# A graph attention layer: one row vector of exponents spread through device memory, and layer normalisation moved to ScalarE

## The chip, the cores and the metric

One core of a Trainium2 chip runs the kernel. The metric is the device time of one execution in microseconds (us), the lower the better. The median of three runs of the kernel before is 437.91 us (437.85 to 437.98). In what follows PE is TensorE, DVE is VectorE, ACT is ScalarE, POOL is GpSimd and SP is SyncE, as the profile writes them.

## The reference

The input is x (4096 nodes, 256 features) and a 4096 x 4096 integer adjacency matrix.

```
h   = relu(layernorm(x))               # over the 256 features, eps 1e-5
h   = h @ W1 + b1                      # 256 x 256
e   = leaky_relu((h @ a1)[:, None] + (h @ a2)[None, :] + b2, 0.2)
att = softmax(where(adj > 0, e, -1e12), axis=1)
out = x + elu(att @ h)
```

## The kernel before

Nodes are cut into 32 tiles of 128. With r from `h @ a1` and p from `h @ a2`, the exponential of the leaky ReLU is, up to a factor of the row that the softmax cancels and a factor u of the column, `max(exp(r), exp(p))`. So the weight of an edge is `adj * max(R, p)`, where R, a row of 4096 values, is needed in the same form in all 128 partitions. Everything is fp32, split for PE into a high and a low part in its fp32r format.

**The head** makes h and its two products. It runs over 8 groups (`GROUPS`) of 4 tiles (`GT`). For a group g:

- DVE takes the statistics of x (`statistics`), POOL forms mean and variance (`moments`), ACT the root (`root`), DVE the reciprocal and the shift (`invert`).
- ACT normalises tiles 0 and 1 of the group and DVE tiles 2 and 3 (`normalise` on both engines, `NORM_ACT = 2`) into `xn`.
- PE transposes the group's 8 blocks into PSUM banks 0 and 1 (`transposes`); ACT applies the ReLU and writes `hnT` (`relu_T`, two halves kc); DVE forms the low part `hnT_lo` from the same banks (`low_T`). The transposes of group g wait for `low_T` of group g - 1, because they write the same banks.
- PE projects with 24 matmuls into banks 2 to 5 (`project`), DVE adds the bias and keeps `h_raw` (`keep_h`, two halves), POOL takes the exponents of r and p from two extra columns into `cr` and `cp` (`exponents`, it raises `c_ready`).
- For R, ACT repeats the four columns of `cr` along the free axis (`repeat_s1`), PE transposes them into bank 6 or 7 (`spread`), so that every partition holds the row, ACT copies them to R (`keep_s`) and later exponentiates 1024 columns of R in place, once for each chunk (`exp_R`).

Each engine runs its own queue in the order written out by hand. ACT's order in iteration g is `relu_T(g+1)`, `normalise(g+2)`, `root(g+3)`, `repeat_s1(g-1)`, `keep_s(g-2)`, with `sign` of pair 1 in iteration 2, the first Exp (of p, and R of chunk 0) in iteration 6 and `high` of pair 0 in iteration 7. DVE's is `invert(g+2)`, `low_T(g+1)`, `normalise(g+2)`, `statistics(g+4)`, `keep_h(g)`, with the sum of hnT (`hsum`, `hsrep`) and `mask(0, 0, 0)` ahead of the last `keep_h`. PE's is `transposes(g)`, `project(g-1)`, `spread(g-2)`.

Then follows **the end phase**: DVE takes the maximum of h @ a2 over all nodes, PE turns it and spreads it (bank 1, then `H0`), ACT forms `u`, and then scales and rounds the tiles of h (`hp_begin`, `scale_h`, `round_h`), with `keep_s(6)` and `keep_s(7)` among them.

**The stream.** Four chunks of 1024 output nodes, in each 16 pairs of source tiles, in rounds of 4 slots. For a pair ACT takes the sign of the adjacency (`sign`, L379), DVE multiplies it with max(R, p) (`mask`, L731), ACT makes the high part `w_hi` (`high`, L387), DVE the low part `w_lo` (`low`, L741), and PE runs 32 matmuls with w_hi and then 16 with w_lo into eight PSUM banks (L600, L602). SP loads one adjacency tile of 1 MB into a slot when its `w_lo` is done. Before the first pair PE opens the sum of each bank with one small matmul (`start_sum`, L576). At the end of a chunk ACT empties the banks, and the output is formed beside the next chunk.

Of the kernel before, what the change touches and what calls it, by code (L numbers as in the profile page):

```python
# [32 lines left out]
P = 128  # L33
# [10 lines left out]
GT = 4  # L44
GROUPS = TILES // GT
NORM_ACT = 2
# [34 lines left out]
def build(nc, adj_t, x, W1, vectors, out):  # L81
# [8 lines left out]
    with ctx:  # L90
# [28 lines left out]
        s1rep = over("s1rep", [P, 2, GT, P], fp32, e_s)  # L119
# [31 lines left out]
        cr = sb("cr", [P, TILES])  # L151
        cp = sb("cp", [P, TILES])
# [3 lines left out]
        H0, S0 = 2, 6  # L156
# [14 lines left out]
        s1_ready = sem("s1_ready")  # L171
# [3 lines left out]
        xn_ready = sem("xn_ready")  # L175
# [5 lines left out]
        s_ready = sem("s_ready")  # L181
        s_kept = sem("s_kept")
# [10 lines left out]
        R_ready = sem("R_ready")  # L193
# [135 lines left out]
        def _(act):  # L329
# [9 lines left out]
            def normalise(g):  # L339

                act.wait_ge(rstd_ready, g + 1)
                if g >= 2:
                    act.wait_ge(tp_ready, KC * (g - 1))
                for t in range(NORM_ACT):
                    tile = g * GT + t
                    last = act.activation(xn[:, g % 2, t, :], x_s[:, tile, :], ACT.Identity,  # L346
                                          scale=rstd[:, tile:tile + 1], bias=shift[:, tile:tile + 1])
                last.then_inc(xn_act, 1)

            def relu_T(g):  # L350

                if g >= 2:
                    act.wait_ge(h_ready, 2 * (g - 1))
                for kc in range(KC):
                    act.wait_ge(tp_ready, KC * g + kc + 1)
                    act.activation(hnT[:, g % 2, kc, :], ps[:, kc, :], ACT.Relu,
                                   accum_out=hs[:, kc, g:g + 1]).then_inc(hn_ready, 1)

            def repeat_s1(g):

                if g >= 2:
                    act.wait_ge(s_ready, g - 1)
                act.wait_ge(c_ready, g + 1)
                act.activation(s1rep[:, g % 2, :, :],
                               cr[:, g * GT:(g + 1) * GT].unsqueeze(2).broadcast_to([P, GT, P]),
                               ACT.Copy).then_inc(s1_ready, 1)

            def keep_s(g):
                act.wait_ge(s_ready, g + 1)
                act.activation(R[:, g * GT * P:(g + 1) * GT * P], ps[:, S0 + g % 2, :], ACT.Copy).then_inc(s_kept, 1)  # L370

            def exp_R(ic):
                part = R[:, ds(ic * CW, CW)]
                act.activation(part, part, ACT.Exp).then_inc(R_ready, 1)
# [22 lines left out]
            for g in range(GROUPS):  # L397
                if g + 1 < GROUPS:
                    relu_T(g + 1)
# [6 lines left out]
                if g >= 1:  # L406
                    repeat_s1(g - 1)
                if g == 6:
# [3 lines left out]
                    act.wait_ge(s_kept, CW // (GT * P))  # L412
                    exp_R(0)
                if g >= 2:
                    keep_s(g - 2)
# [4 lines left out]
            repeat_s1(GROUPS - 1)  # L420
# [39 lines left out]
            def round_of(ic, r, first, last):  # L460
                inner = r is not FIRST_ROUND and r is not LAST_ROUND
                for c in range(SLOTS):
# [14 lines left out]
                    if r is FIRST_ROUND and c == 2 and not last:  # L477
                        exp_R(ic + 1)
# [14 lines left out]
            keep_s(GROUPS - 2)  # L493
            keep_s(GROUPS - 1)
            act.wait_ge(s_kept, GROUPS)
# [10 lines left out]
        def _(pe):  # L506
            def transposes(g, u):

                pe.wait_ge(xn_ready, g + 1)
                pe.wait_ge(xn_act, g + 1)  # L510
                for kc in range(KC):
                    if at_least(g, 1):
                        pe.wait_ge(hn_lo_ready, (g - 1) * KC + kc + 1)
                    for t in range(GT):
                        last = pe.transpose(ps[:, kc, t * P:(t + 1) * P], xn[:, u, t, kc * P:(kc + 1) * P],  # L515
                                            ident[:, :])
# [16 lines left out]
            def spread(g, u):  # L533

                pe.wait_ge(s1_ready, g + 1)
                if at_least(g, 2):
                    pe.wait_ge(s_kept, g - 1)
                for t in range(GT):
                    last = pe.transpose(ps[:, S0 + u, t * P:(t + 1) * P], s1rep[:, u, t, :], ident[:, :])
                last.then_inc(s_ready, 1)  # L540

# [7 lines left out]
            spread(0, 0)  # L549
            transposes(3, 1)  # L550
            project(2, 0)
            spread(1, 1)
# [13 lines left out]
            spread(GROUPS - 2, 0)  # L566
# [11 lines left out]
            def pair(ic, m, b, first, begin=False):  # L578

                n = ic * PAIRS + m  # L580
                for part, w in ((0, w_hi), (1, w_lo)):
                    pe.wait_ge((hi_ready, lo_ready)[part], n + 1)
                    for s in range(2):
# [7 lines left out]
                        for ib in range(BANKS):  # L591
                            acc = ps[:, ib, 0:HW].unsqueeze(1)
                            block_w = w[:, b, s, ib * P:(ib + 1) * P]
                            if begin and part == 0 and s == 0 and not (first and ib < S0):
                                if first:
                                    pe.wait_ge(s_kept, GROUPS + ib - S0 - 1)
                                else:
                                    pe.wait_ge(evacuated, (ic - 1) * BANKS + ib + 1)
                                start_sum(ib)
# [34 lines left out]
            for ib in range(S0):  # L634
# [6 lines left out]
        def _(dve):  # L641
# [26 lines left out]
            def normalise(g):  # L668

                if g >= 2:  # L670
                    dve.wait_ge(tp_ready, KC * (g - 1))
                for t in range(NORM_ACT, GT):
                    tile = g * GT + t
                    last = dve.tensor_scalar(xn[:, g % 2, t, :], x_s[:, tile, :], mean[:, tile:tile + 1],  # L674
                                             rstd[:, tile:tile + 1], ALU.subtract, ALU.mult)
                last.then_inc(xn_ready, 1)

            def low_T(g):
# [3 lines left out]
                for kc in range(KC):  # L682
                    dve.wait_ge(hn_ready, KC * g + kc + 1)
                    dve.scalar_tensor_tensor(hnT_lo[:, g % 2, kc, :], ps[:, kc, :], 0.0,  # L684
# [62 lines left out]
            normalise(0)  # L747
            weights()
            invert(1)
            normalise(1)  # L750
# [5 lines left out]
            for g in range(GROUPS):  # L756
# [6 lines left out]
                if g + 2 < GROUPS:  # L763
                    normalise(g + 2)
# [7 lines left out]
                if g == 7:  # L772
# [7 lines left out]
                    dve.wait_ge(R_ready, 1)  # L780
# [48 lines left out]
            def round_of(ic, r, first, last):  # L829
                inner = r is not FIRST_ROUND and r is not LAST_ROUND  # L830
                for c in range(SLOTS):
# [10 lines left out]
                    if r is LAST_ROUND and c == 0 and not last:  # L842
                        dve.wait_ge(R_ready, ic + 2)
# [58 lines left out]
```

## Time and profile before

| | |
|---|---|
| median of 3 runs | 437.91 us |
| the profiled execution | 437.82 us |
| its span, first to last instruction | 436.0 us |
| PE busy | 413.6 us (95%), 3399 matmuls |
| DVE busy | 375.9 us (86%) |
| ACT busy | 315.9 us (72%) |
| POOL busy | 24.1 us (6%) |
| PE: L600 and L602, matmuls of the stream | 592.4 us as summed durations, which overlap |
| DMA | 80.60 MB, 185 GB/s on average |

The profile shows one execution. The busy share of an engine is an average over the head (to about 57 us), the stream and a short tail (from about 431 us). Durations of matmuls in a row overlap, so their pace is read from their start times or from a count in a stretch. ACT's and DVE's operations overlap their successors by about 0.1 us in the same way.

### The profile page before, as it was taken

How to read it: one execution, taken by the hardware profiler on the slowest of the kernel's cores; microseconds unless marked ns; L12 is line 12 of the kernel's file. 1: busy time of each engine (PE TensorE's matmuls, PEld its weight loads, DVE VectorE, ACT ScalarE, POOL GpSimd, SP SyncE). 2: the span in 40 equal slices, each digit the busy share in tenths (PEclk: the TensorE clock that was granted, in tenths of full speed). 3: DMA queues.
4: the chain of work that ended last, by engine and by line, in shares of the span. 5: the costliest groups of instructions: out<-in, count | busy, mean ns of one | idle time of the engine just before them, and what ended most of it. 6: DMA issues, size and time to landing. Idle time of an engine off the chain costs nothing.

```text
span 436.0 us, 8665 instructions
## 1 busy us (share of the span) xinstructions
PE 413.6 (95%) x3399; PEld 410.2 (94%) x3399; DVE 375.9 (86%) x403; ACT 315.9 (72%) x312; POOL 24.1 (6%) x95
## 2 busy tenths in 40 slices
PE   0799979999999999999999999999999999999995
PEld 0789979999999999999999999999999999999995
DVE  3999899999999389999996399999991799999905
ACT  2678899999996298958663799758562989576503
POOL 2333200000000000000000000000000000000005
PEclk9999999999999999999999999999999999999999
DMA  7940015555555725638478155747576256475302
GB/s 269 384 180 1 0 52 208 193 213 207 192 193 194 289 98 200 246 135 275 159 260 305 64 192 201 259 150 266 148 261 254 85 204 229 156 252 229 96 0 96
DMA packets 22355, 80.60 MB, mean 185 GB/s; under 512 B 1472, under 2 KB 14016, under 8 KB 14144
## 3 DMA queue, kind: packets, MB, share of 16 engines
q1 hardware_dynamic: 21920, 79.70, 51.6%
q10 hardware_dynamic: 416, 0.66, 0.5%
q8 instruction: 11, 0.18, 0.2%
q14 instruction: 8, 0.07, 0.0%
HBM read 76.15 MB, written 4.19 MB: 184 GB/s over the span
## 4 chain that ended last, share of the span: by engine, by line
PE 87%; DVE 8%; ACT 2%; DMA 2%; issue 1%; POOL 0%; POOLq 0%; SPq 0%; DVEq 0%; ACTq 0%
PE ps L600 52%; PE ps L602 26%; DVE stats L657 2%; DMA x_s<-x 2%; PE ps L618 1%; PE ps L616 1%; PE ps L617 1%; DVE hnT_lo L684 1%; PE ps L527 1%; DVE h_raw L693 1%; PE ps L529 1%; PE ps L528 1%; DVE y L878 1%; DVE xn L674 1%; PE ps L576 1%; PE ps L515 1%
## 5 line engine op out<-in xcount | busy, mean ns | idle before, releaser
L600 PE MATMUL ps<-hp_hi,w_hi 128*128 (+1 forms) x960 | 233.6, 282 | 0.9 <-ACT w_hi L387 0.9
L602 PE MATMUL ps<-hp_lo,w_hi 128*128 (+1 forms) x960 | 233.6, 282 | 0.0
L731 DVE SCALAR_TENSOR_TENSOR adj_s<-R,p,adj_s 128x1024 f32<-128x1024 f32 x128 | 158.2, 1276 | 31.7 <-ACT adj_s L379 31.7
L600 PEld LDWEIGHTS ps<-hp_hi,w_hi 128*128 128x128 f32 x960 | 181.3, 189 | 1.2 <-ACT w_hi L387 1.1
L602 PEld LDWEIGHTS ps<-hp_lo,w_hi 128*128 128x128 f32 x960 | 181.1, 189 | 0.0
L387 ACT ACTIVATE w_hi<-adj_s 128x2048 fp32r<-128x2048 f32 x64 | 122.4, 1913 | 33.5 <-DVE adj_s L731 33.0
L741 DVE SCALAR_TENSOR_TENSOR w_lo<-adj_s,w_hi 128x2048 fp32r<-128x2048 f32 x64 | 146.1, 2283 | 0.4 <-ACT w_hi L387 0.3
L379 ACT ACTIVATE adj_s<-adj_s 128x2048 f32<-128x2048 int32 x64 | 122.4, 1912 | 19.4 <-DMA adj_s<-adj_t 18.8
L600 PE MATMUL ps<-hp_hi,w_lo 128*128 (+1 forms) x960 | 125.2, 283 | 0.6 <-DVE w_lo L741 0.6
L600 PEld LDWEIGHTS ps<-hp_hi,w_lo 128*128 128x128 f32 x960 | 119.4, 189 | 0.8 <-DVE w_lo L741 0.8
L451 ACT ACTIVATE y<-ps 128x258 f32<-128x258 f32 x24 | 9.3, 387 | 28.1 <-PE ps L618 28.1
L326 POOL TENSOR_TENSOR adj_s<-y,adj_s 128x256 f32<-128x256 f32 x8 | 5.7, 709 | 373.0 <-DVE y L878 372.7
L515 PE MATMUL ps<-ident,xn 128*128 128x128 f32 x64 | 10.2, 312 | 13.7 <-ACT xn L346 11.2
L515 PEld LDWEIGHTS ps<-ident,xn 128*128 128x128 f32 x64 | 8.5, 161 | 14.4 <-issue 11.4
L527 PE MATMUL ps<-W_hi,hnT 128*128 128x258 f32 x64 | 19.7, 308 | 0.8 <-DVE h_raw L693 0.6
L529 PE MATMUL ps<-W_hi,hnT_lo 128*128 128x258 f32 x64 | 18.9, 295 | 0.0
L528 PE MATMUL ps<-W_lo,hnT 128*128 128x258 f32 x64 | 18.9, 295 | 0.0
L618 PE MATMUL ps<-hp_hi,w_lo 128*128 128x258 f32 x64 | 18.0, 282 | 0.0
L616 PE MATMUL ps<-hp_hi,w_hi 128*128 128x258 f32 x64 | 18.0, 281 | 0.0
L617 PE MATMUL ps<-hp_lo,w_hi 128*128 128x258 f32 x64 | 18.0, 281 | 0.0
L657 DVE BATCH_NORM_STATS2 stats<-x_s 128x6 f32<-128x256 f32 x32 | 11.2, 412 | 5.9 <-DMA x_s<-x 5.9
L503 ACT ACTIVATE y<-ps,rden 128x256 f32<-128x256 f32 x8 | 3.8, 475 | 15.9 <-DVE rden L867 15.9
(89 smaller groups left out, 273.9 us busy)
## 6 DMA issues: line engine op xcount, KB each, us to landing
adj_s<-adj_t SPq DMA_DIRECT2D x64, 1024.0 KB, 4.8
x_s<-x SPq DMA_DIRECT2D x8, 512.0 KB, 10.2
o_s<-x SPq DMA_DIRECT2D x3, 1024.0 KB, 7.7
out<-o_s SPq DMA_DIRECT2D x6, 512.0 KB, 6.9
adj_s<-x SPq DMA_DIRECT2D x1, 1024.0 KB, 5.5
out<-adj_s SPq DMA_DIRECT2D x8, 128.0 KB, 1.7
vec<-vectors ACTq DMA_DIRECT2D x1, 384.5 KB, 6.4
W1x<-W ACTq DMA_DIRECT2D x1, 256.0 KB, 4.8
```

Source lines behind the costliest of these rows:

```text
L379: act.activation(adj_w[:, c, :, :], adj_s[:, c, :, :], ACT.Sign).then_inc(signed, 1)
L387: act.activation(w_hi[:, c, :, :], adj_w[:, c, :, :], ACT.Relu).then_inc(hi_ready, 1)
L515: last = pe.transpose(ps[:, kc, t * P:(t + 1) * P], xn[:, u, t, kc * P:(kc + 1) * P], ident[:, :])
L527: pe.matmul(acc, hnT[:, u, kc, node], W_hi[:, kc, :], start=kc == 0, stop=False)
L528: pe.matmul(acc, hnT[:, u, kc, node], W_lo[:, kc, :], start=False, stop=False)
L529: last = pe.matmul(acc, hnT_lo[:, u, kc, node], W_hi[:, kc, :], start=False, stop=kc == KC - 1)
L600: last = pe.matmul(acc, block_w, hh, start=False, stop=False)
L602: pe.matmul(acc, block_w, hl, start=False, stop=False)
L616: pe.matmul(acc, w_hi[:, b, s, col], hh, start=False, stop=False)
L617: pe.matmul(acc, w_hi[:, b, s, col], hl, start=False, stop=False)
L731: last = dve.scalar_tensor_tensor(sgn, R[:, ds(ic * CW, CW)], p[:, ds(source(r, c) + s, 1)], sgn, ALU.max, ALU.mult)
L741: dve.scalar_tensor_tensor(w_lo[:, c, :, :], adj_w[:, c, :, :], 0.0, w_hi[:, c, :, :].bitcast(fp32), ALU.max, ALU.subtract).then_inc(lo_re ...
```

## The change

R is no longer built in 8 steps in all partitions. PE turns 16 columns of `cr` (128 x 16) into 16 rows of 128 with one transpose (`turn_r`, twice), ACT exponentiates these 16 x 128 values (`exp_r`), and SP stores them as 8 KB to a tensor in device memory and loads them back to all 128 partitions, 1 MB (`spread`, now on SP). `repeat_s1`, `keep_s`, `exp_R` and PE's `spread` are gone. The first half is turned on PE between `project(4)` and `transposes(6)`, and PE waits there for `exp_r(0)`, which ACT does at the start of iteration 5; the second half is turned beside the maximum. `mask(0, 0, 0)` waits for the load of the first half. ACT normalises all four tiles of a group, DVE none. The transposes use banks 0 and 1 for even groups and 6 and 7 for odd ones, and wait for `low_T` of group g - 2. The loop over groups on PE is written out, and all eight sums are opened ahead of the first pair.

```diff
-NORM_ACT = 2
+HALF_T = TILES // 2
...
-        s1rep = over("s1rep", [P, 2, GT, P], fp32, e_s)
...
+        r_row = [sb(f"r_row{k}", [HALF_T, P]) for k in range(2)]
+        r_rows = nc.dram_tensor("r_rows", (TILES, P), fp32, kind="Internal").ap()
...
-        H0, S0 = 2, 6
+        H0 = 2
+        T0 = (0, 6)
+        RB = (1, 6)
...
+            def spread(k):
+                tiles = slice(k * HALF_T, (k + 1) * HALF_T)
+                sp.wait_ge(r_ready, k + 1)
+                sp.dma_start(r_rows[tiles, :], r_row[k][:, :]).then_inc(r_out, 16)
+                sp.wait_ge(r_out, (k + 1) * 16)
+                sp.dma_start(R[:, k * HALF_T * P:(k + 1) * HALF_T * P],
+                             r_rows[tiles, :].rearrange("t p -> (t p)").partition_broadcast(P)).then_inc(R_in, 16)
+            spread(0)
+            spread(1)
...
-                for t in range(NORM_ACT):
+                for t in range(GT):
                     tile = g * GT + t
                     last = act.activation(xn[:, g % 2, t, :], x_s[:, tile, :], ACT.Identity,
...
-                    act.activation(hnT[:, g % 2, kc, :], ps[:, kc, :], ACT.Relu,
+                    act.activation(hnT[:, g % 2, kc, :], ps[:, T0[g % 2] + kc, :], ACT.Relu,
...
-            def repeat_s1(g):
-            def keep_s(g):
-            def exp_R(ic):
...
+            def exp_r(k):
+                act.wait_ge(rT_ready, k + 1)
+                act.activation(r_row[k][:, :], ps[0:HALF_T, RB[k], 0:P], ACT.Exp).then_inc(r_ready, 1)
...
             for g in range(GROUPS):
+                if g == 5:
+                    exp_r(0)
                 if g + 1 < GROUPS:
                     relu_T(g + 1)
...
-                if g >= 1:
-                    repeat_s1(g - 1)
                 if g == 6:
                     act.wait_ge(c_ready, EARLY // GT)
                     act.activation(p[:, 0:EARLY], cp[:, 0:EARLY], ACT.Exp).then_inc(p_ready, 1)
-                    act.wait_ge(s_kept, CW // (GT * P))
-                    exp_R(0)
-                if g >= 2:
-                    keep_s(g - 2)
...
-            repeat_s1(GROUPS - 1)
+            exp_r(1)
+            act.wait_ge(c_ready, GROUPS)
             act.activation(p[:, EARLY:TILES], cp[:, EARLY:TILES], ACT.Exp).then_inc(p_ready, 1)
...
-                    if r is FIRST_ROUND and c == 2 and not last:
-                        exp_R(ic + 1)
...
-            keep_s(GROUPS - 2)
-            keep_s(GROUPS - 1)
-            act.wait_ge(s_kept, GROUPS)
...
-                pe.wait_ge(xn_ready, g + 1)
                 pe.wait_ge(xn_act, g + 1)
                 for kc in range(KC):
-                    if at_least(g, 1):
-                        pe.wait_ge(hn_lo_ready, (g - 1) * KC + kc + 1)
+                    if at_least(g, 2):
+                        pe.wait_ge(hn_lo_ready, (g - 2) * KC + kc + 1)
...
-            def spread(g, u):
...
+            def turn_r(k):
+                pe.wait_ge(c_ready, (k + 1) * HALF_T // GT)
+                pe.transpose(ps[0:HALF_T, RB[k], 0:P], cr[:, k * HALF_T:(k + 1) * HALF_T], ident[:, :]).then_inc(rT_ready, 1)
...
-            with pe.Fori(2, GROUPS // 2) as k:
+            for k in range(2, GROUPS // 2):
                 transposes(2 * k, 0)
                 project(2 * k - 1, 1)
-                spread(2 * k - 2, 0)
                 transposes(2 * k + 1, 1)
                 project(2 * k, 0)
-                spread(2 * k - 1, 1)
+                if k == 2:
+                    turn_r(0)
+                    pe.wait_ge(r_ready, 1)
...
             pe.transpose(ps[0:1, 1, 0:P], gm[:, 0:1], ident[:, :]).then_inc(pmaxT_ready, 1)
+            turn_r(1)
             pe.wait_ge(g1_ready, 1)
             pe.matmul(ps[:, H0, 0:1], ones[0:1, 0:P], gm[0:1, 1:2], start=True, stop=True).then_inc(g_ps, 1)
-            spread(GROUPS - 1, 1)
...
             pe.wait_ge(prep_done, 1)
-            for ib in range(S0):
+            pe.wait_ge(r_ready, 2)
+            for ib in range(BANKS):
                 start_sum(ib)
...
-            def normalise(g):
...
-                    dve.wait_ge(R_ready, 1)
+                    dve.wait_ge(R_in, 16)
                     mask(0, 0, 0)
...
-                    if r is LAST_ROUND and c == 0 and not last:
-                        dve.wait_ge(R_ready, ic + 2)
+                    if first and r is LAST_ROUND and c == 0:
+                        dve.wait_ge(R_in, 32)
```

The first part of the diff is in `build`, then come SP's queue (`spread`), ACT's, PE's and DVE's.

## Rows read from the trace of the kernel before

**Rows 1.** Stretches: length, busy us of PE, PEld, DVE, ACT, POOL, clock, DMA share, GB/s.

```profile
30.00:40.00 10.00, 9.68 (x79) 8.99 (x78) 9.78 (x26) 9.15 (x22) 3.87 (x20) 1.00 0.00 1
...
70.00:430.00 360.00, 360.00 (x3007) 360.00 (x3006) 313.60 (x249) 263.97 (x212) 2.05 (x3) 1.00 0.55 193
...
433.00:436.00 3.00, 0.00 (x0) 0.00 (x0) 0.13 (x1) 0.00 (x0) 0.84 (x2) 0.68 0.39 131
```

**Rows 2.** Waits over the span: who for whom, total us, times, longest.

```profile
ACT hnT L356 <- PE ps L515: 5.1, 5, 1.5
```

**Rows 3.** Timeline, 11 to 23 us: start, length, operation, idle time before it.

```profile
11.93 0.30 ACT L336 ACTIVATE std<-var,eps 128x4 f32<-128x4 f32 x1 [0.85 <-POOL var L304]
...
13.76 0.57 ACT L356 ACTIVATE hnT<-ps 128x512 fp32r<-128x512 f32 x1
...
21.02 1.09 ACT L346 ACTIVATE xn<-x_s,shift,rstd 128x256 f32<-128x256 f32 x2 [1.70 <-DVE shift L665]
...
21.57 0.28 PE L529 MATMUL ps<-W_hi,hnT_lo 128*128 128x258 f32 x1
22.01 0.28 ACT L336 ACTIVATE std<-var,eps 128x4 f32<-128x4 f32 x1
...
22.20 1.07 PE L515 MATMUL ps<-ident,xn 128*128 128x128 f32 x8 [0.36 <-issue]
...
22.93 0.60 ACT L356 ACTIVATE hnT<-ps 128x512 fp32r<-128x512 f32 x1 [0.64 <-PE ps L515]
```

**Rows 4.** Timeline of VectorE, groups 2 and 3.

```profile
24.34 1.29 DVE L684 SCALAR_TENSOR_TENSOR hnT_lo<-ps,hnT 128x512 fp32r<-128x512 f32 x2
25.54 0.73 DVE L674 TENSOR_SCALAR xn<-x_s,mean,rstd 128x256 f32<-128x256 f32 x2
...
28.98 1.29 DVE L684 SCALAR_TENSOR_TENSOR hnT_lo<-ps,hnT 128x512 fp32r<-128x512 f32 x2
```

**Rows 5.** Timeline of ScalarE, 31 to 60 us.

```profile
31.28 1.90 ACT L379 ACTIVATE adj_s<-adj_s 128x2048 f32<-128x2048 int32 x1
33.08 0.58 ACT L356 ACTIVATE hnT<-ps 128x512 fp32r<-128x512 f32 x1
...
34.22 1.09 ACT L346 ACTIVATE xn<-x_s,shift,rstd 128x256 f32<-128x256 f32 x2
...
48.06 1.28 ACT L411 ACT_TABLE_LOAD   x1
49.35 0.22 ACT L411 ACTIVATE p<-cp 128x24 f32<-128x24 f32 x1
49.48 1.05 ACT L374 ACTIVATE R<-R 128x1024 f32<-128x1024 f32 x1
...
58.07 1.05 ACT L370 ACTIVATE R<-ps 128x512 f32<-128x512 f32 x2
```

**Rows 6.** Timelines of TensorE, VectorE and GpSimd, 45 to 66 us.

```profile
45.56 1.04 PE L515 MATMUL ps<-ident,xn 128*128 128x128 f32 x8
...
50.73 2.48 DVE L731 SCALAR_TENSOR_TENSOR adj_s<-R,p,adj_s 128x1024 f32<-128x1024 f32 x2
...
54.91 0.23 POOL L312 TENSOR_SCALAR cp<-h_raw 128x4 f32<-128x4 f32 x1
...
55.36 0.38 PE L571 MATMUL ps<-gm,ones 1*128 1x1 f32 x2 [0.37 <-DVE gm L787]
...
62.53 2.19 PE L600 MATMUL ps<-hp_hi,w_lo 128*128 128x258 f32 x16 [0.61 <-DVE w_lo L741]
...
65.59 0.39 PE L600 MATMUL ps<-hp_hi,w_hi 128*128 128x258 f32 x1 [0.86 <-ACT w_hi L387]
```

**Rows 7.** DMA issues: queue, number, KB of one, us from issue to landing.

```profile
adj_s<-adj_t SPq DMA_DIRECT2D x64, 1024.0 KB, 4.8
x_s<-x SPq DMA_DIRECT2D x8, 512.0 KB, 10.2
...
out<-adj_s SPq DMA_DIRECT2D x8, 128.0 KB, 1.7
```

More of the change, by code:

```diff
@@ L170, in build @@
         const_ready = sem("const_ready")
-        s1_ready = sem("s1_ready")
         var_ready = sem("var_ready")
@@ L174, in build @@
         xn_act = sem("xn_act")
-        xn_ready = sem("xn_ready")
         tp_ready = sem("tp_ready")
@@ L180, in build @@
         h_kept = sem("h_kept")
-        s_ready = sem("s_ready")
-        s_kept = sem("s_kept")
         hsrep_ready = sem("hsrep_ready")
@@ L192, in build @@
         u_ready = sem("u_ready")
-        R_ready = sem("R_ready")
+        rT_ready = sem("rT_ready")
+        r_ready = sem("r_ready")
+        r_out = sem("r_out")
+        R_in = sem("R_in")
         ones_col = sem("ones_col")
@@ L355, in relu_T @@
                     act.wait_ge(tp_ready, KC * g + kc + 1)
-                    act.activation(hnT[:, g % 2, kc, :], ps[:, kc, :], ACT.Relu,
+                    act.activation(hnT[:, g % 2, kc, :], ps[:, T0[g % 2] + kc, :], ACT.Relu,
                                    accum_out=hs[:, kc, g:g + 1]).then_inc(hn_ready, 1)
-            def repeat_s1(g):
-                if g >= 2:
[L362 to L366, printed above, removed]
-            def keep_s(g):
-                act.wait_ge(s_ready, g + 1)
-                act.activation(R[:, g * GT * P:(g + 1) * GT * P], ps[:, S0 + g % 2, :], ACT.Copy).then_inc(s_kept, 1)
-            def exp_R(ic):
-                part = R[:, ds(ic * CW, CW)]
-                act.activation(part, part, ACT.Exp).then_inc(R_ready, 1)
+            def exp_r(k):
+                act.wait_ge(rT_ready, k + 1)
+                act.activation(r_row[k][:, :], ps[0:HALF_T, RB[k], 0:P], ACT.Exp).then_inc(r_ready, 1)
             def sign(ic, r, c):
@@ L411, in _ @@
                     act.activation(p[:, 0:EARLY], cp[:, 0:EARLY], ACT.Exp).then_inc(p_ready, 1)
-                    act.wait_ge(s_kept, CW // (GT * P))
-                    exp_R(0)
-                if g >= 2:
-                    keep_s(g - 2)
                 if g == 7:
@@ L507, in transposes @@
             def transposes(g, u):
-                pe.wait_ge(xn_ready, g + 1)
                 pe.wait_ge(xn_act, g + 1)
                 for kc in range(KC):
-                    if at_least(g, 1):
-                        pe.wait_ge(hn_lo_ready, (g - 1) * KC + kc + 1)
+                    if at_least(g, 2):
+                        pe.wait_ge(hn_lo_ready, (g - 2) * KC + kc + 1)
                     for t in range(GT):
-                        last = pe.transpose(ps[:, kc, t * P:(t + 1) * P], xn[:, u, t, kc * P:(kc + 1) * P],
+                        last = pe.transpose(ps[:, T0[u] + kc, t * P:(t + 1) * P], xn[:, u, t, kc * P:(kc + 1) * P],
                                             ident[:, :])
@@ L531, in project @@
                         last.then_inc(h_ready, 1)
-            def spread(g, u):
[L535 to L540, printed above, removed]
             pe.wait_ge(pool_c, 3)
@@ L548, in _ @@
             project(1, 1)
-            spread(0, 0)
             transposes(3, 1)
             project(2, 0)
-            spread(1, 1)
-            with pe.Fori(2, GROUPS // 2) as k:
+            def turn_r(k):
+                pe.wait_ge(c_ready, (k + 1) * HALF_T // GT)
+                pe.transpose(ps[0:HALF_T, RB[k], 0:P], cr[:, k * HALF_T:(k + 1) * HALF_T], ident[:, :]).then_inc(rT_ready, 1)
+            for k in range(2, GROUPS // 2):
                 transposes(2 * k, 0)
                 project(2 * k - 1, 1)
-                spread(2 * k - 2, 0)
                 transposes(2 * k + 1, 1)
                 project(2 * k, 0)
-                spread(2 * k - 1, 1)
+                if k == 2:
+                    turn_r(0)
+                    pe.wait_ge(r_ready, 1)
             project(GROUPS - 1, 1)
@@ L565, in _ @@
             last.then_inc(hsum_ps, 1)
-            spread(GROUPS - 2, 0)
             pe.wait_ge(pmax_ready, 1)
             pe.transpose(ps[0:1, 1, 0:P], gm[:, 0:1], ident[:, :]).then_inc(pmaxT_ready, 1)
+            turn_r(1)
             pe.wait_ge(g1_ready, 1)
             pe.matmul(ps[:, H0, 0:1], ones[0:1, 0:P], gm[0:1, 1:2], start=True, stop=True).then_inc(g_ps, 1)
-            spread(GROUPS - 1, 1)
             def start_sum(ib):
@@ L593, in pair @@
                             block_w = w[:, b, s, ib * P:(ib + 1) * P]
[L594 to L598, printed above, removed]
+                            if begin and part == 0 and s == 0 and not first:
+                                pe.wait_ge(evacuated, (ic - 1) * BANKS + ib + 1)
                                 start_sum(ib)
@@ L666, in invert @@
                     .then_inc(rstd_ready, 1)
-            def normalise(g):
[L670 to L676, printed above, removed]
             def low_T(g):
@@ L683, in low_T @@
                     dve.wait_ge(hn_ready, KC * g + kc + 1)
-                    dve.scalar_tensor_tensor(hnT_lo[:, g % 2, kc, :], ps[:, kc, :], 0.0,
+                    dve.scalar_tensor_tensor(hnT_lo[:, g % 2, kc, :], ps[:, T0[g % 2] + kc, :], 0.0,
                                              hnT[:, g % 2, kc, :].bitcast(fp32), ALU.max, ALU.subtract)\
@@ L746, in _ @@
             invert(0)
-            normalise(0)
             weights()
             invert(1)
-            normalise(1)
             split_weights()
@@ L762, in _ @@
                     invert(2)
-                if g + 2 < GROUPS:
-                    normalise(g + 2)
                 if g + 4 < GROUPS:
```

## The prediction

> **What bounds the kernel now.** I read the stretches first [rows 1]. From 70 to 430 us TensorE is busy for 360.00 of 360.00 us, so nothing that relieves ScalarE or VectorE there can shorten the span, and the matmuls of that part are not changed. What can move is the moment at which the pair stream starts without a gap, which is the head. The head ends with two short gaps in front of the stream [rows 6]: 0.61 us until VectorE's w_lo at 62.53, 0.86 us until ScalarE's w_hi at 65.59. From 65.59 on TensorE never waits. So the question is: when does the matmul at 65.59 (pair 1, its w_hi part) start after the change? Everything behind it moves by the same amount.
>
> In the head, 30 to 40 us has VectorE at 9.78, TensorE at 9.68 and ScalarE at 9.15 of 10 us [rows 1]: all three are near full, so I follow the pitch of the groups. VectorE's low_T(2) starts at 24.34 and low_T(3) at 28.98, 4.64 us apart [rows 4], with no idle time of VectorE named in either row: VectorE sets the pace there. ScalarE has waits in between, 5.1 us in 5 times, all for the transposes [rows 2].
>
> **What the change takes away.** VectorE loses its two tiles of normalise, about 0.65 us of each group (0.73 for two overlapping [rows 4]); its pitch would be 3.99. TensorE loses four transposes a group and ScalarE two passes (repeat_s1, keep_s). In the end phase ScalarE loses keep_s(6) and keep_s(7), 1.05 us [rows 5], which lie between u and w_hi of pair 1. The exp_R passes of the later chunks lie beside a full TensorE: nothing. At the head of chunk 0, exp_R(0) (1.05 us [rows 5]) is beside VectorE's work and is not waited for: nothing.
>
> **What it adds, and where.** ScalarE now normalises four tiles, 1.98 instead of 0.99 us (21.02 to 22.01 for two [rows 3]), and it does so between relu_T(g+1) and the transposes of g+2, for which it then waits. That is a ring: transposes start; relu_T starts 0.73 us later (22.20 to 22.93 [rows 3]); relu_T takes 1.14 (33.08 to 34.22 [rows 5]); the transposes start 1.18 us after a two-tile normalise starts (21.02 to 22.20 [rows 3]), so 2.17 after a four-tile one. Sum 0.73 + 1.14 + 2.17 = 4.04 us. This is a hair above VectorE's 3.99, so ScalarE's ring becomes the pace, and nothing in it has slack: whatever else stands in ScalarE's queue there is paid in full.
>
> Entry. relu_T(0) starts at 13.76, right behind normalise(1) [rows 3]; two more tiles put it, and VectorE's low_T(0) that waits for it, 0.99 late. normalise(0) costs nothing more: its two further tiles fill a wait of 0.85 us in front of root(1) [rows 3] and end about when that starts. From there VectorE is without a gap until the shift that releases normalise(2) at 21.02 (nothing of what it does there is removed: its normalise(0) and (1) lie before low_T(0), normalise(2) behind that shift), so normalise(2) starts at 22.01 and the transposes of group 2 at 22.01 + 2.17 = 24.18 instead of 22.20 [rows 3]. The two new banks let transposes(1) start before low_T(0), but project(0) comes no earlier for that, since it needs all of low_T(0), which is late; and nothing waits for it, since TensorE will stand idle in front of the transposes of group 2: no gain, no loss.
>
> Then the ring. Group 3 at 28.22, group 4 at 32.26. In iteration 2 ScalarE also does sign of pair 1, 1.80 us [rows 5] (31.28 to 33.08), which before fell mostly into its waits. Now: normalise(4) from 28.22 + 0.73 + 1.14 = 30.09 to 32.08, root(5) 0.2, sign to 34.09, where relu_T(4) would otherwise start at 32.99: 1.1 us paid. Group 5: 34.09 + 1.14 + 2.17 = 37.40.
>
> Then exp_r(0). TensorE turns the first 16 columns after project(4) and waits for r_ready before the transposes of group 6. ScalarE's order is relu_T(5), normalise(6), root(7), then exp_r(0), and exp_r(0) is now the first Exp, so the table load that stood before the exponent of p (48.06, 1.28 us [rows 5]) stands here. normalise(6) runs from 39.27 to 41.26, root(7) ends 41.54 (0.28 as in [rows 3]), the load 42.82, exp_r(0) about 0.31 us (between 0.22 for 24 columns and 1.05 for 1024, 0.00083 us a column [rows 5]) to 43.13, and TensorE starts at 43.25. Without it group 6 would start at 37.40 + 4.04 = 41.44: 1.8 us paid. Whether the load comes before or after the wait matters little: turning is done at 41.3 + 0.3 = 41.6 and ScalarE reaches the load at 41.54. Group 7: 43.25 + 4.04 = 47.29, against 45.56 [rows 6]. From the relief of VectorE there is a gain of only 0.25 us between groups 2 and 7 (45.56 - 22.20 = 23.36 before, 47.29 - 24.18 = 23.11 after), because sign and exp_r(0) eat it. The head is 1.73 us late here.
>
> The Trainium skill, "ScalarE: Activation LUTs", section "What ACT_TABLE_LOAD costs", puts a switch of table sets at 1.28 us and another 1.38 us of drain. The trace has p's ACTIVATE at 49.35, 0.01 us behind the load's end [rows 5], so it shows no such drain; by the page the sum would be 1.4 us more.
>
> R through device memory. r_ready 43.2; a store of 8 KB, bounded by the 128 KB stores at 1.7 us; then 1 MB to 128 partitions, as the adjacency tiles, 4.8 us [rows 7]: R_in at about 49.9 with issue. Bounds: 0 for the store and 4.8, or 1.7 and 10.2 (the x loads while the queues were full [rows 7]), 48.0 to 55.2. mask(0,0,0) wants it at 50.73 + 1.73 = 52.46 [rows 6]. The queues carry 1 GB/s at 30 to 40 us [rows 1], so I take 4.8, the row of the same shape, 8 KB to each of 128 partitions: hidden with 2.6 us to spare. The second half is wanted by chunk 2 only; in SP's queue it stands ahead of load_adj(4), which waits for the same w_lo as TensorE at 62.53 [rows 6], 1.8 later; store and load are issued at 57.6 and over by about 64.3 (57.6 + 1.7 + 4.8 and the issue), so the tile isn't held up. Nothing.
>
> End phase. From the transposes of group 7 to mask(0,0,0), keep_h(7) and the maximum the order is unchanged, all 1.73 late. turn_r(1) now waits on TensorE for cp of POOL (ends 55.14) and is ahead of the matmul that spreads the maximum (55.36) [rows 6]: 0.2 us of room for an issue of 0.1 to 0.2, I take 0.05. exp_r(1) and the second p fit before u. Then ScalarE's way to w_hi of pair 1 is shorter by 1.05: 65.59 + 1.78 - 1.05 = 66.32. TensorE itself: w_lo of pair 0 at 62.53 + 1.78 = 64.31, and 16 matmuls of 0.12 (360 us for 3007 [rows 1]) to 66.23. The later of them, 66.32, is 0.73 after 65.59. Eight sums opened at once instead of six: same count, TensorE waits for w_lo there anyway.
>
> Sum: 1.98 (entry) - 0.25 (ring, with sign and the table load inside) + 0.05 - 1.05 = +0.73 us. The profiled execution took 437.82 us (span 436.0), 0.09 below the median of 437.91. 437.91 + 0.73 = 438.64; I say 438.6. About 0.2% (0.88 us, 437.03 to 438.79) is what a measurement of this kernel can tell from no change, and the sum lies just inside.
>
> **Rivals.**
> A. As worked: 438.1 to 439.2, from 0.2 to 0.3 us of error at each of entry, sign and exp_r. Chance 0.62.
> B. Faster: ScalarE's ring is not the pace. If a four-tile normalise let the transposes start tile by tile, or the latencies were shorter so that the ring fell under 3.99, VectorE's relief would count in the four groups that still have statistics: 4 x 0.65 = 2.6. With +1.0 at the entry, +1.4 for the table load and -1.05: 436.7; with the table load hidden too, 435.3. For it: VectorE is the pace now [rows 4], ScalarE shows waits [rows 2]. Against: these waits are the latency of the ring, not room, and xn_act is signalled once, after the fourth tile. It decides if the ring takes under 3.99 us. Chance 0.12.
> C. R is late: it decides once store and load take more than 9.2 us together. At the upper bound (55.2) mask(0,0,0) is 2.7 us late: 441.3. Chance 0.08.
> D. TensorE's clock falls. Between project(0), over by 21.6, and the transposes of group 2 it now stands idle for 2.6 us (0.4 before: 21.85 to 22.20 [rows 3]). The one fall that the trace has is behind the last matmul: the granted clock of 433 to 436 us is 0.68 on average [rows 1], so it went to 1.2 GHz within about 3 us of idleness. At the lower level project(1) takes up to twice its 24 matmuls of 0.12, 2.9 us, which holds back group 3: +1.5 to +2.7, so 440.1 to 441.3. Against it: 2.6 is less than that idleness. Chance 0.09.
> E. The page's drain behind the table load: the load in the ring costs 1.38 more, 440.0. Chance 0.02, since the row speaks against it.
> The rest, 0.07, is a wait of 0.3 to 1 us that I haven't seen.
>
> **Range and chances.** A alone reaches 438.1 to 439.2. To leave out no more than 2 in 10 I go down to 437.2 (into B) and up to 440.4 (into D, E and the nearer part of C). Slower by over 0.2%: a good third of A (its centre is 0.15 under the border), C, D, E and most of the rest: 0.43. Faster by over 0.2%: most of B, 0.10. Within: 0.47.
>
> **What would show it.** In the profile after: transposes of group 2 start near 24.2 with TensorE idle 2.6 us before them; groups 3 and 4 follow at 4.0 us; groups 4 to 5 at 5.1, 5 to 6 at 5.8 with a table load in front of exp_r(0) and TensorE waiting for it about 1.8 us; VectorE waits for ScalarE's hnT in each group; no wait of mask(0,0,0) for a transfer; the gap before w_hi of pair 1 nearly gone while the one before w_lo of pair 0 stays. Wrong if the groups follow at under 3.9 us, if mask waits for R, or if the matmuls of project(1) take clearly more than the 0.28 of [rows 3].

## The result and the profile after

The changed kernel takes 440.13 us (440.06 to 441.15, 4 runs), the kernel before 437.95 us beside it. The ratio is 1.0056, with a 95% interval of 1.0044 to 1.0068: slower by 2.2 us. I had said 438.6, slower by 0.7 us.

TensorE's timeline shows where the head lost it. The rows with x8 are the transposes of groups 2 to 7; the first and the last of them answer to the ones at 22.20 [rows 3] and 45.56 [rows 6] of the kernel before.

```profile
20.46 0.28 PE L522 MATMUL ps<-W_hi,hnT_lo 128*128 128x258 f32 x1
24.17 1.09 PE L508 MATMUL ps<-ident,xn 128*128 128x128 f32 x8 [3.43 <-ACT xn L360]
...
25.49 0.42 PE L520 MATMUL ps<-W_hi,hnT 128*128 128x258 f32 x1
...
29.50 1.04 PE L508 MATMUL ps<-ident,xn 128*128 128x128 f32 x8
...
33.48 1.09 PE L508 MATMUL ps<-ident,xn 128*128 128x128 f32 x8
...
38.59 1.09 PE L508 MATMUL ps<-ident,xn 128*128 128x128 f32 x8 [1.13 <-ACT xn L360]
...
44.40 1.09 PE L508 MATMUL ps<-ident,xn 128*128 128x128 f32 x8 [1.73 <-ACT r_row L376]
...
48.44 1.09 PE L508 MATMUL ps<-ident,xn 128*128 128x128 f32 x8
```

Group 2 starts at 24.17 us, against the 24.18 that I had worked out. But TensorE has then been idle for 3.43 us, not 2.6, and the matmuls of project(1) behind it change from 0.28 us at 25.22 to 0.42 us at 25.49. Group 3 follows 5.33 us after group 2 instead of 4.04. Groups 3 to 7 keep to the sum: 3.98, 5.11 (with sign), 5.81 (with the table load and exp_r(0)), 4.04. Group 7 starts at 48.44; I had 47.29.

The stretches of the same execution (columns as in [rows 1], the clock is the figure after the engines' counts):

```profile
20.00:25.00 5.00, 1.57 (x15) 1.36 (x14) 4.73 (x14) 2.63 (x7) 2.62 (x15) 1.00 1.02 424
25.00:29.00 4.00, 4.00 (x23) 4.00 (x22) 3.19 (x7) 3.34 (x9) 1.16 (x7) 0.57 0.37 152
29.00:59.00 30.00, 25.02 (x199) 23.27 (x197) 22.48 (x54) 20.38 (x46) 9.02 (x39) 1.00 0.10 37
...
60.00:63.00 3.00, 3.00 (x15) 3.00 (x15) 3.00 (x4) 2.97 (x7) 0.00 (x0) 0.51 0.66 259
```

The granted clock is 0.57 on average from 25 to 29 us and 0.51 from 60 to 63 us. So TensorE went to 1.2 GHz twice before the stream ran full, the first time behind its 3.43 us of idleness, the second time at the eight sums (`h_tiny`) that open pair 0. From 29 to 59 us it had 2.4 GHz.

ScalarE's rows bear out the terms that concern it: relu_T(0) at 14.78 (14.75 worked out), the table load of 1.28 us in front of exp_r(0), and 0.27 us for exp_r.

```profile
14.78 0.57 ACT L370 ACTIVATE hnT<-ps 128x512 fp32r<-128x512 f32 x1
...
42.78 1.28 ACT L376 ACT_TABLE_LOAD   x1
44.08 0.27 ACT L376 ACTIVATE r_row<-ps 16x128 f32<-16x128 f32 x1
```

R was no problem. The issues (KB of one, us to landing), SP's issues and VectorE's first mask are:

```profile
R<-r_rows SPq DMA_DIRECT2D x2, 1024.0 KB, 4.5
...
r_rows<-r_row SPq DMA_DIRECT2D x2, 8.0 KB, 1.3
```

```profile
45.74 0.34 SPq L259 DMA_DIRECT2D R<-r_rows  x1
...
60.08 0.32 SPq L259 DMA_DIRECT2D R<-r_rows  x1
65.48 0.34 SPq L235 DMA_DIRECT2D adj_s<-adj_t  x1
```

```profile
53.65 2.47 DVE L706 SCALAR_TENSOR_TENSOR adj_s<-R,p,adj_s 128x1024 f32<-128x1024 f32 x2
```

The first load is issued at 45.74, 1.39 us after the end of exp_r(0), and lands some 4.5 us later, at about 50.3. mask(0,0,0) starts at 53.65 without a wait. The second load is issued at 60.08; the adjacency load behind it in SP's queue follows at 65.48, over 5 us later, so it is not held up by it.

The end phase, first the kernel before (TensorE's timeline), then the changed one:

```profile
53.51 0.60 PE L539 MATMUL ps<-ident,s1rep 128*128 128x128 f32 x4
...
55.92 0.66 PE L539 MATMUL ps<-ident,s1rep 128*128 128x128 f32 x4 [0.19 <-ACT s1rep L364]
```

```profile
57.63 0.27 PE L556 MATMUL ps<-ident,gm 128*1 128x128 f32 x1 [1.48 <-DVE gm L756]
...
59.69 2.09 PE L563 MATMUL ps<-h_tiny,ones 128*128 128x258 f32 x8 [0.99 <-DVE h_tiny L770]
...
66.02 2.08 PE L584 MATMUL ps<-hp_hi,w_lo 128*128 128x258 f32 x16
```

Before, the old spreads of R (0.60 and 0.66 us) lay ahead of the maximum and behind it. In the changed kernel TensorE is idle for 1.48 and 0.99 us there, and the eight sums of h_tiny behind the second gap take 2.09 us. w_lo of pair 0 is used from 66.02 on, where before it was 62.53 [rows 6], and there is no gap in front of it, because TensorE had not finished with w_hi.

### The profile page after: what moved, and what is told of

Its sections match the earlier page's. It is cut to its first block, busy times and chain, and to the rows that moved or that the text cites. A ratio compares the mean times of both kernels' runs of the same rounds, so it can differ in the third digit from the quotient of the medians.

```text
span 438.3 us, 8557 instructions
## 1 busy us (share of the span) xinstructions
PE 411.1 (94%) x3369; PEld 408.4 (93%) x3369; DVE 371.1 (85%) x387; ACT 312.3 (71%) x310; POOL 24.1 (6%) x95
## 4 chain that ended last, share of the span: by engine, by line
PE 87%; ACT 5%; DVE 4%; DMA 2%; issue 1%; POOL 0%; POOLq 0%; SPq 0%; ACTq 0%; DVEq 0%
PE ps L584 53%; PE ps L586 26%; ACT xn L360 3%; DMA x_s<-x 2%; PE ps L600 1%; PE ps L602 1%; PE ps L601 1%; ACT hnT L370 1%; PE ps L508 1%; PE ps L563 1%; DVE stats L642 1%; DVE y L849 1%; PE ps L522 1%; DVE hnT_lo L659 1%; PE ps L520 1%
## 5 line engine op out<-in xcount | busy, mean ns | idle before, releaser
L360 ACT ACTIVATE xn<-x_s,shift,rstd 128x256 f32<-128x256 f32 x32 | 16.6, 594 | 3.2 <-DVE shift L650 3.2
L659 DVE SCALAR_TENSOR_TENSOR hnT_lo<-ps,hnT 128x512 fp32r<-128x512 f32 x16 | 10.3, 685 | 7.1 <-ACT hnT L370 6.1
```

## The experiments

All of them take the changed kernel as their base, apart from one. A filling is a row of transposes of the identity into a PSUM bank that nobody reads at that time; it adds nothing to the result. All fillings use this function:

```diff
+            def fill(bank, n):
+                for _ in range(n):
+                    pe.transpose(ps[:, bank, 0:P], ident[:, :], ident[:, :])
```

**The gap before group 2 filled.**

```diff
             project(0, 0)
+            fill(0, 24)
             transposes(2, 0)
```

> The changed kernel with 24 more 128x128 transposes of the identity into bank 0 between project(0) and transposes(2); they add nothing to the result. Clock theory: the 1.3 us by which group 3's transposes came later than the worked 4.04 us behind group 2's is TensorE at 1.2 GHz, after 3.4 us of idleness. With the gap filled the clock stays at 2.4 GHz, groups 2 to 3 are 4.0 to 4.1 us apart, and the time falls by 1.2 us to about 438.9. Rival (ring only: ScalarE's four-tile normalise sets the pace whatever TensorE's clock is): groups 2 to 3 stay at about 5.3 us, time 440.1 as before. If the 24 transposes themselves are in the way, the transposes of group 2 start later than 24.17 us.

Measured: 439.58 us (438.68 to 440.64, 7 runs), ratio 1.0033 (1.0022 to 1.0045). In the profiled execution, the slowest of the seven, groups 2 to 3 are 28.11 - 24.07 = 4.04 us apart and group 7 starts at 47.08, so the first fall is gone, as the clock theory says, and the rival fails. The time fell by 0.55 us in the median and not by 1.2. Most of the difference lies outside the span, the time from the first instruction to the last. The median span fell from 438.3 to 437.1 us, which is the 1.2. But these runs take 2.0 to 2.8 us beyond their span, and those of the changed kernel and of the kernel before 1.7 to 1.9. Why, no run shows. The second fall still comes, and in the profiled execution it is longer than in the changed kernel's:

```profile
25.00:30.00 5.00, 4.92 (x43) 4.71 (x42) 4.36 (x11) 4.38 (x13) 2.00 (x11) 1.00 0.30 120
...
55.00:60.00 5.00, 2.52 (x11) 2.13 (x12) 4.02 (x13) 4.30 (x9) 0.64 (x3) 0.74 0.09 26
60.00:65.00 5.00, 5.00 (x28) 5.00 (x28) 5.00 (x5) 5.00 (x8) 0.00 (x0) 0.58 0.45 185
```

**The gaps of the end phase filled.**

```diff
             last.then_inc(hsum_ps, 1)
+            fill(7, 18)
...
             pe.matmul(ps[:, H0, 0:1], ones[0:1, 0:P], gm[0:1, 1:2], start=True, stop=True).then_inc(g_ps, 1)
+            fill(7, 8)
```

> The changed kernel with 18 transposes of the identity into bank 7 behind the matmuls of hsum and 8 behind the one that spreads the maximum. Clock theory: the granted clock, 0.50 from about 59.8 to 63.0 us, stays at 1.00, the first matmuls of pair 0 follow at 0.12 instead of 0.21 us, pair 1 starts 0.3 to 0.6 us earlier, time about 439.7. Rival (pair 1 is bound by ScalarE's and VectorE's chain from u, so TensorE's clock under pair 0 costs nothing): 440.1.

Measured: 441.23 us (439.92 to 441.31, 4 runs), ratio 1.0077 (1.0060 to 1.0093). Both theories missed: one run is at 439.9 and three are at 441.2 to 441.3. The profiled execution is the fastest of the four. Its clock holds from 55 us on, but it falls at the first gap, and earlier than in the changed kernel. TensorE was idle for 2.56 us there and already has 1.2 GHz when the transposes of group 2 start (1.97 us for the eight, and a clock of 0.50):

```profile
24.02 1.97 PE L508 MATMUL ps<-ident,xn 128*128 128x128 f32 x8 [2.56 <-ACT xn L360]
```

```profile
24.00:25.00 1.00, 0.97 (x5) 0.98 (x6) 0.62 (x3) 0.16 (x1) 0.85 (x5) 0.50 1.00 418
25.00:30.00 5.00, 5.00 (x36) 5.00 (x35) 3.80 (x8) 3.55 (x10) 1.52 (x9) 0.78 0.29 118
...
55.00:60.00 5.00, 4.81 (x37) 4.05 (x36) 3.76 (x12) 3.15 (x6) 0.64 (x3) 1.00 0.01 2
```

The three slower runs have no trace, only their mean granted clock over the span: 0.989 to 0.992, against 0.995 for the profiled one. The changed kernel has such a run too (441.15, with 0.988 against 0.992 for its other three). More time at 1.2 GHz may go with them, but the mean alone does not show it: the kernel before has means of 0.993 to 0.999 in runs of 437.8 to 438.4 us. Also, 18 transposes were too many: they ended after the maximum was ready, and held TensorE's work on it back by 0.3 us.

**Both filled.** The two edits together.

> Both fillings in one kernel. Clock theory: the gains add, 1.2 + 0.4, time 438.4 to 438.6, which is the sum that was worked out for the change without any fall of the clock. Rival (ring only): 440.1. If the second fall is one consequence of the first (its gap moved with it), the gain is that of the first filling alone, 438.9.

Measured: 438.91 us (438.80 to 439.10, 10 runs), ratio 1.0023 (1.0014 to 1.0033). The scatter of 1 to 2 us is gone as well. It is 0.3 us above the upper end of what was expected, as much as the filling that was too long costs; the next experiment tests that.

**The fillings fitted.** 24, 12 and 8 transposes.

> The changed kernel with its three gaps of TensorE filled by 24, 12 and 8 transposes of the identity; the middle filling is six shorter than in the first such kernel, where it held the maximum back by 0.3 us. It tests the worked sum of the prediction by itself, without any fall of the clock: 0.73 us above the kernel before, so 438.5 to 438.8. If the sum was wrong in its own terms and two errors hid each other, the time is outside 438.3 to 439.0.

Measured: 438.59 us (438.45 to 438.80, 11 runs), the kernel before 437.89 beside it, ratio 1.0016 (1.0007 to 1.0025): 0.70 us slower, against a worked sum of 0.73. TensorE's rows, groups 2 to 7 and then w_lo of pair 0:

```profile
24.21 1.09 PE L508 MATMUL ps<-ident,xn 128*128 128x128 f32 x8 [0.82 <-ACT xn L360]
...
28.24 1.09 PE L508 MATMUL ps<-ident,xn 128*128 128x128 f32 x8
...
32.28 1.09 PE L508 MATMUL ps<-ident,xn 128*128 128x128 f32 x8
...
37.39 1.09 PE L508 MATMUL ps<-ident,xn 128*128 128x128 f32 x8 [1.14 <-ACT xn L360]
...
43.19 1.09 PE L508 MATMUL ps<-ident,xn 128*128 128x128 f32 x8 [1.72 <-ACT r_row L376]
...
47.22 1.09 PE L508 MATMUL ps<-ident,xn 128*128 128x128 f32 x8
```

```profile
64.29 2.18 PE L592 MATMUL ps<-hp_hi,w_lo 128*128 128x258 f32 x16 [0.76 <-DVE w_lo L724]
```

The steps are 4.03, 4.04, 5.11, 5.80 and 4.03 us. Worked out were 24.18, 28.22, 32.26, 37.40, 43.25 and 47.29 for the groups and 64.31 for w_lo.

**Two tiles on VectorE again.** `normalise` is back on both engines for each group; R and the four banks stay changed.

```diff
+def on_act(g):
+    return GT // 2
...
-                for t in range(GT):
+                for t in range(on_act(g)):
...
+            def normalise(g):
+                if on_act(g) == GT:
+                    return
+                if g >= 2:
+                    dve.wait_ge(tp_ready, KC * (g - 1))
+                for t in range(on_act(g), GT):
+                    tile = g * GT + t
+                    last = dve.tensor_scalar(xn[:, g % 2, t, :], x_s[:, tile, :], mean[:, tile:tile + 1],
+                                             rstd[:, tile:tile + 1], ALU.subtract, ALU.mult)
+                last.then_inc(xn_ready, 1)
```

> One part of the change undone: VectorE normalises tiles 2 and 3 of every group again, ScalarE tiles 0 and 1; R still goes through device memory and the transposes keep four banks. Theory (four tiles in ScalarE's ring cause both the late entry and the gap in which the clock falls): transposes of group 2 at 22.2 us, VectorE the pace at 4.64 us a group, group 7 at 45.4 to 45.8, exp_r with its table load nearly hidden, pair 1 at about 64.4 to 64.9, time 436.7 to 437.3, faster than the kernel before by the two copies of R that have left the end phase. Rival (the loss is exp_r and the wait of TensorE for it in the middle of the groups): group 5 to 6 stays at 5.8 us and the time at 438.5 or more.

Measured: 437.12 us (436.62 to 438.14, 10 runs), ratio 0.9987 (0.9977 to 0.9996). Group 2 starts at 22.44, groups 3 to 5 follow 4.4 to 4.7 us apart and group 6 5.36 us behind group 5, TensorE waits 0.46 us for exp_r(0) instead of 1.73, and group 7 starts at 45.35. So the four tiles in ScalarE's queue are the loss, and exp_r alone is not. The clock holds behind a gap of 2.02 us in front of group 2 and falls in the end phase:

```profile
22.44 1.07 PE L516 MATMUL ps<-ident,xn 128*128 128x128 f32 x8 [2.02 <-DVE xn L669]
```

```profile
25.00:30.00 5.00, 4.35 (x37) 4.14 (x37) 4.97 (x14) 2.91 (x9) 2.37 (x13) 1.00 0.30 121
...
55.00:60.00 5.00, 4.02 (x21) 3.81 (x22) 4.42 (x12) 4.42 (x11) 0.00 (x0) 0.66 0.37 152
```

**The same with the end phase filled** (12 and 8 transposes).

> The kernel with two tiles each on ScalarE and VectorE (R through device memory, four banks), and 12 and 8 transposes of the identity into bank 7 in TensorE's two gaps of the end phase. In the kernel without them the granted clock of 55 to 60 us was 0.66. Clock theory: it stays at 1.00, pair 1 starts 0.3 to 0.6 us earlier, 436.5 to 436.7, and the runs scatter less. Rival (TensorE's clock there costs nothing, the chain behind u decides): 437.1 with the same scatter.

Measured: 436.66 us (436.51 to 436.72, 7 runs), ratio 0.9969 (0.9957 to 0.9980), with a scatter of 0.2 instead of 1.5 us (on another chip than the run without fillings, beside 437.99 and 437.93 of the kernel before). The clock theory holds here too, and the gap of 2.33 us in front of group 2, which is not filled, is not followed by a fall:

```profile
22.20 1.07 PE L516 MATMUL ps<-ident,xn 128*128 128x128 f32 x8 [2.33 <-DVE xn L676]
```

```profile
55.00:60.00 5.00, 5.00 (x41) 4.79 (x42) 4.42 (x9) 4.63 (x11) 0.00 (x0) 1.00 0.40 156
```

**Only the normalisation moved, in the kernel before.**

```diff
-NORM_ACT = 2
+NORM_ACT = 4
...
-                pe.wait_ge(xn_ready, g + 1)
                 pe.wait_ge(xn_act, g + 1)
```

VectorE's `normalise` and its calls are gone.

> One part of the change done alone in the kernel before: ScalarE normalises all four tiles; R is still built with repeat_s1, spread and keep_s, and the transposes have two banks. Ring theory: ScalarE's queue per group is 1.14 + 1.98 + 0.2 + 0.52 + 0.48 = 4.3 us with no room, group 2 at 24.2, group 7 near 47.7, which is 2.1 late; with a fall of the clock in the gap before group 2 another 0.5 to 1.3 us. Time 440.0 to 441.4. Rival (the loss comes from the new way of R: its table load, its waits): time within 0.5 us of the kernel before, since VectorE is relieved.

Measured: 443.48 us (443.42 to 444.20, 4 runs), ratio 1.0131 (1.0114 to 1.0148). The direction was right, but the size was not: 5.5 us instead of 2 to 3.5 over the kernel before (437.99 beside it). Groups 2 to 3 take 5.23 us and 3 to 4 take 5.18, with the clock at 1.00 in both:

```profile
24.12 1.09 PE L514 MATMUL ps<-ident,xn 128*128 128x128 f32 x8 [1.56 <-ACT xn L346]
...
28.86 0.66 PE L538 MATMUL ps<-ident,s1rep 128*128 128x128 f32 x4 [0.76 <-ACT s1rep L364]
29.35 1.04 PE L514 MATMUL ps<-ident,xn 128*128 128x128 f32 x8
...
34.03 0.66 PE L538 MATMUL ps<-ident,s1rep 128*128 128x128 f32 x4 [0.77 <-ACT s1rep L364]
34.53 1.04 PE L514 MATMUL ps<-ident,xn 128*128 128x128 f32 x8
```

TensorE waits 0.76 us for s1rep in front of the old spread, and the transposes of the next group stand behind that in its queue. repeat_s1 comes behind ScalarE's normalise. So here the ring is 0.75 (transposes to relu_T) + 1.16 (relu_T) + 1.97 (normalise) + 0.19 (root) + 0.67 (repeat_s1, to the start of the old spread) + 0.49 (from there to the transposes) = 5.23 us, from the start times of this trace. I had added up ScalarE's queue alone, 4.3 us, and left out the legs over TensorE. From group 2 to group 7 it takes 51.20 - 24.12 = 27.08 us, against 23.36 before: 3.72. With 1.92 at the entry that is 5.64, and the profiled executions are 443.42 - 437.82 = 5.60 us apart. In the end phase the clock falls in this execution too (0.50 from 63 to 65 us), behind gaps of 0.60, 0.37 and 0.19 us, the same as in the trace of before, where it stayed up. It costs nothing there: w_hi of pair 1 follows 71.17 - 51.20 = 19.97 us behind group 7, and 20.03 before.

**sign of pair 1 out of the ring**, in the changed kernel with the fitted fillings.

```diff
                 if g == 6:
                     act.wait_ge(c_ready, EARLY // GT)
                     act.activation(p[:, 0:EARLY], cp[:, 0:EARLY], ACT.Exp).then_inc(p_ready, 1)
+                    sign(0, 0, 1)
...
-                if g == 2:
-                    sign(0, 0, 1)
```

> The changed kernel with four tiles on ScalarE, TensorE's gaps filled (24, 12 and 8 transposes of the identity), and sign of pair 1 moved from iteration 2 to behind the first exponent of p in iteration 6, where ScalarE was idle for 5.6 us. Ring theory (whatever stands in ScalarE's queue between two groups is paid in full): groups 4 to 5 go from 5.10 to 4.04 us and the time falls by 1.1 us from 438.6 (the kernel with fillings, less the 0.3 us by which its filling was too long) to 437.5. Rival (VectorE's 3.99 us a group takes over, so that the gain is cut to less than half): 438.1 or more.

Measured: 437.62 us (437.50 to 437.73, 10 runs), ratio 0.9991 (0.9982 to 1.0001). That is 0.97 us less than the 438.59 of the fitted kernel (the two ran on different chips, beside 437.99 and 437.89 of the kernel before; measured from these it is 0.37 us faster against 0.70 slower, 1.07 in all). Groups 4 to 5 take 4.03 us:

```profile
32.34 1.09 PE L507 MATMUL ps<-ident,xn 128*128 128x128 f32 x8
...
36.37 1.09 PE L507 MATMUL ps<-ident,xn 128*128 128x128 f32 x8
...
42.18 1.09 PE L507 MATMUL ps<-ident,xn 128*128 128x128 f32 x8 [1.73 <-ACT r_row L376]
```

**Tiles split by group.** `on_act(g)` is 4 for groups 3, 4 and 5 and 2 for the others; sign as above; 12 and 8 transposes in the end phase.

> Two tiles on ScalarE in groups 0, 1, 2, 6 and 7, four in groups 3, 4 and 5; sign of pair 1 in iteration 6; 12 and 8 transposes of the identity in the end phase. Ring theory: group 2 at 22.4 us with no gap before it, then about 4.04 us a group instead of 4.64, group 7 near 43.5, time 434.6 to 435.4. Rival (VectorE stays the pace because its work for the first two groups and the bias keeps it behind): group 7 at 45 or later, 436.3 or more.

Measured: 435.68 us (434.85 to 436.48, 4 runs), ratio 0.9941 (0.9922 to 0.9960), in two pairs: 434.9 and 436.5. The profiled execution is of the slower pair. TensorE was idle for 2.45 us before group 2 at 22.36, where I had expected no gap, and group 3 follows 5.94 us later:

```profile
22.36 1.06 PE L515 MATMUL ps<-ident,xn 128*128 128x128 f32 x8 [2.45 <-DVE xn L675]
...
28.30 1.04 PE L515 MATMUL ps<-ident,xn 128*128 128x128 f32 x8
```

```profile
25.00:30.00 5.00, 5.00 (x34) 5.00 (x34) 3.85 (x11) 2.87 (x8) 2.38 (x13) 0.73 0.31 128
```

**The same with the first gap filled** (`fill(0, 12)`).

> The version that the other runs point to: two tiles on ScalarE in groups 0, 1, 2, 6, 7, four in 3, 4, 5; sign of pair 1 in iteration 6; R through device memory; 12, 12 and 8 transposes of the identity in TensorE's gaps. The same kernel without the first filling came out at 434.9 or at 436.5, with groups 2 to 3 5.9 us apart and the clock at 0.73 from 25 to 30 us in a run of the slower kind. Clock theory: every run at 434.8 to 435.2, groups 2 to 3 at 4.3 to 4.5 us. Rival (the two levels have another cause than the clock in that gap): the runs stay spread between 434.9 and 436.5.

Measured: 434.62 us (434.58 to 434.78, 5 runs), ratio 0.9927 (0.9913 to 0.9941), 3.3 us faster than the kernel before. All five runs are together, 0.02 to 0.22 us below the expected 434.8; the step between groups 2 and 3 is 4.45 us. So the two levels came from this gap.

```profile
22.18 1.06 PE L515 MATMUL ps<-ident,xn 128*128 128x128 f32 x8 [1.06 <-DVE xn L676]
...
26.63 1.04 PE L515 MATMUL ps<-ident,xn 128*128 128x128 f32 x8
```

## Why the prediction was wrong

- **The step that failed** is the treatment of rival D. The sum took TensorE's clock as given, and "2.6 is less than that idleness" was the reason for a chance of 0.09. The trace after shows the clock fall behind that gap, and the filling shows that the gap was the cause. The time lay 2.18 us above the kernel before, 1.45 more than the sum's 0.73. Filling the gaps gives 1.54 back (440.13 to 438.59) and leaves 0.70. Rival D had the mechanism, but the time within its 440.1 to 441.3 is in part luck: it priced the first fall alone at 1.5 or more, which measured 1.2, and it had no second fall.
- **Two things in that step were off.** The first is the idle time, 3.43 and not 2.6 us (with the 21.85 of [rows 3] for the end of project(0) it would even have been 2.3). The matmuls of project(0) change from 0.42 to 0.28 us each at about 18.6 us, where in the trace of before they did so at 20.9, and so they ended at 20.7. The profile's clock column has 1.00 there in both traces, so that the lower pace at the start is seen in the matmuls alone. The second is the comparison. A gap of 2.56 us in front of group 2 was followed by 1.2 GHz with only the end phase filled, and one of 2.45 us in the mixed split, so the 2.6 us would have been no safety either. The single fall in the trace of before gave no lower bound for the idle time that it takes.
- **The price of each fall.** In the profiled executions the first fall puts group 7 at 48.44 instead of 47.22, 1.2 us later, and w_hi of pair 1 then comes at 67.94 instead of 66.39: 0.3 more from the second. The median spans say the same: 438.3 us with both, 437.1 with the first gap filled, 436.8 with all. But the second alone lasted longer in the profiled execution with the first gap filled, and w_hi of pair 1 came at 67.75 there, 20.67 us behind group 7 instead of 19.17: 1.5.
- **The second fall was not foreseen at all.** I had taken the old spreads of R off TensorE in the end phase and counted the room as free. Idle for 1.48 and 0.99 us there, TensorE opens pair 0 at 1.2 GHz: the eight sums of h_tiny take 2.09 us, and 1.23 with the gaps filled. With two tiles on each engine, filling these gaps alone is worth 437.12 - 436.66 = 0.46 us in the median, and up to 1.5 in single runs.
- **Entry: right.** 24.18 worked out, 24.17 measured. No gain from the two banks here: with the old banks and four tiles on ScalarE group 2 starts at 24.12.
- **The ring: right.** 4.04 worked out, 4.03 to 4.04 measured, and sign costs 1.07 in it (5.11 - 4.04; taken out, the time falls by 0.97). Rival B is out: VectorE's 3.99 never becomes the pace.
- **Table load and exp_r: right.** 5.80 against 5.85 worked out. The rival of a drain behind the load (the Trainium skill, "ScalarE: Activation LUTs", "What ACT_TABLE_LOAD costs") is out for this kernel: exp_r(0) starts at 44.08, 0.02 us behind the load's end at 44.06.
- **R through device memory: hidden**, with 3.3 us to spare (2.6 worked out; mask(0,0,0) was itself 1.2 us later than worked out). Rival C is out.
- **End phase: right in size.** w_lo of pair 0 at 64.29, worked out 64.31, once the clock stays up. As worked, pair 1 waits for TensorE's own 16 matmuls or for w_hi, which come within 0.1 us of each other.
- **What I did not see about the change as a whole:** its parts have opposite signs. The new way of R, together with the four banks, which no run takes apart, is worth 1.3 us with two tiles on each engine (436.66, with the gaps of its end phase filled); moving the other two tiles to ScalarE then costs 1.9 us (438.59), and 1.5 more by the clock. But the move alone, with the old way of R, costs 5.5.

What stays open: which executions fall, and for how long. Of the runs of 441.2 us with only the end phase filled, and of the one of 441.15 of the changed kernel, no trace exists, only a span that is longer by 1.1 to 1.4 us and a lower mean clock. Where in the span that goes is not shown.

## What to carry to other kernels

When a change takes work from TensorE or delays what it waits for, list its idle gaps before and after, and price each gap that the change opens as if the clock might fall behind it (here 1.2 us for the one at the entry, and 0 to 1.5 for those of the end phase); useless transposes in the gap are a cheap test of that, and sometimes the cure. Before moving work from a saturated engine to one with waits, write down the ring in which these waits lie: if they are the latency of a hand-over within the ring that sets the pace, the work is paid in full. Two edits that are made together may be worth undoing one at a time, since one may carry the other.

## What was unexpected of the hardware

Gaps of TensorE of 2.0 to 3.4 us in front of group 2, between stretches of full work, did not all end the same way. In the profiled executions 1.2 GHz followed gaps of 3.43, 2.56 and 2.45 us, and did not follow gaps of 2.33 and 2.02 us. The length alone does not decide: in the mixed split the profiled execution with its 2.45 us took 436.48 us (granted clock 0.73 from 25 to 30 us), and so did one of the three others, but two took 434.9.

Nor does the fall always come at the same place. In the changed kernel the matmuls are at full pace until 25.4, 1.2 us after work was taken up again at 24.17, and at the lower pace until 28.7. With only the end phase filled the clock is already at 0.50 when work is taken up at 24.02, and the lower pace ends at 27.1.

The scatter goes with it. The runs of the five kernels with fillings whose profiled execution shows no fall lie within 0.2 to 0.4 us of each other. In the six changed kernels whose profiled execution shows one they are 0.8 to 2.0 us apart, of which a part lies outside the span for the entry filling alone.
